# The fifth mixing product in one pass of fp32r over exact high and low parts, with the tanh values in the keys' buffer

## What is computed

```python
xx = x_prev - x
mix = jnp.tanh((x + xx * time_maa_x) @ maa_w1).reshape(b, t, 5, E_MIX)   # E_MIX = 32
mix = jnp.einsum('btfe,fec->fbtc', mix, maa_w2)
mw, mk, mv, mr, mg = mix
xw = x + xx * (time_maa_w + mw)      # likewise xk, xv, xr, xg
r = xr @ Wr.T;  k = xk @ Wk.T;  v = xv @ Wv.T
g = jax.nn.silu(xg @ Wg.T)
```

## Time and profile before

| what | us |
|---|---|
| median of 3 runs (lowest, highest) | 3530.97 (3509.68, 3533.42) |
| the profiled execution: time, span | 3509.35, 3507.2 |
| TensorE, VectorE, ScalarE, GpSimd busy | 3143.1, 2473.1, 1897.2, 784.9 |
| mean granted clock of TensorE | 0.983 |
| keys' buffer K1 in one tile: last read (state product, L542) starts | 1749.80 |
| tanh values are written to TMA (L782), TMB (L784) | 1764.16, 1766.00 |
| keys are written to K1 again (L653) | 1790.41 |
| setup: GpSimd's subtraction over two weight blocks (L847) takes | 2.40 |

### The profile page before, as it was taken

One profiled execution on the slowest core, in us unless ns is written; L12 is line 12 of the kernel. 1 busy time (PEld: TensorE's weight loads), 2 busy tenths in 40 slices (PEclk: granted clock), 3 DMA queues, 4 the chain that ended last, 5 costly groups with the idle time before them and its releaser, 6 DMA issues.

```text
span 3507.2 us, 98753 instructions
## 1 busy us (share of the span) xinstructions
PE 3143.1 (90%) x39261; PEld 2257.9 (64%) x39261; DVE 2473.1 (71%) x5108; ACT 1897.2 (54%) x3852; POOL 784.9 (22%) x725
## 2 busy tenths in 40 slices
PE   1899999999999999999999999999999999999997
PEld 0566666766666766666666666766666766666764
DVE  8466686776676676776766776676786776677776
ACT  0445556645566555566555566555566655556653
POOL 3122211122221122221222221222211122221121
PEclk9899999999999999999999999999999999999998
DMA  4000000000000000000000000000000000000000
GB/s 184 14 8 19 20 14 17 17 14 20 14 17 20 17 14 20 14 17 20 17 14 20 14 17 20 17 14 20 14 19 18 17 20 14 20 14 17 20 17 13
DMA packets 22598, 73.04 MB, mean 21 GB/s; under 512 B 3041, under 2 KB 3297, under 8 KB 20545
## 3 DMA queue, kind: packets, MB, share of 16 engines
q1 hardware_dynamic: 22208, 66.76, 5.4%
HBM read 49.97 MB, written 16.78 MB: 19 GB/s over the span
## 4 chain that ended last, share of the span: by engine, by line
PE 25%; DVE 22%; issue 21%; ACT 19%; POOL 10%; POOLq 1%; DMA 1%; ACTq 1%; DVEq 0%; SPq 0%
PE psP L393 7%; ACT ARENA L653 7%; PE psP L423 6%; ACT HHI L810 6%; POOL MT L856 5%; POOL ARENA L870 4%; PE psF L615 4%; ACT GG L801 3%; DVE ARENA L1125 3%; DVE ARENA L1087 3%; DVE ARENA L1077 2%; DVE HLO L1237 2%; DVE SUMS L1229 2%; DVE GR L1245 2%; PE psX L375 1%
## 5 line engine op out<-in xcount | busy, mean ns | idle before, releaser
L393 PE MATMUL psP<-ARENA,WALL 128*128 128x256 f32 x3072 | 692.0, 382 | 0.2 <-ACT ARENA L684 0.2
L653 ACT ACTIVATE ARENA<-ARENA 32x512 f32<-32x512 f32 (+1 forms) x992 | 578.8, 583 | 189.8 <-DVE ARENA L1077 137.7
L393 PEld LDWEIGHTS psP<-ARENA,WALL 128*128 128x128 f32 x3072 | 574.6, 190 | 84.5 <-issue 11.3
L1237 DVE SCALAR_TENSOR_TENSOR HLO<-GG,FWB,HHI 128x128 f16<-128x128 f32 x1024 | 292.3, 347 | 459.8 <-ACT HHI L810 455.7
L615 PE MATMUL psF<-XHI,WFC 128*128 128x128 f16 x4096 | 490.0, 220 | 46.5 <-DVE XLO L1216 34.0
L615 PE MATMUL psF<-XLO,WFC 128*128 128x128 f16 x4096 | 488.8, 220 | 0.0
L615 PEld LDWEIGHTS psF<-XHI,WFC 128*128 128x128 f16 x4096 | 401.7, 99 | 88.1 <-issue 86.0
L615 PEld LDWEIGHTS psF<-XLO,WFC 128*128 128x128 f16 x4096 | 402.9, 98 | 14.0 <-issue 10.3
L870 POOL TENSOR_TENSOR ARENA<-ARENA,XT 128x1024 f32<-128x1024 f32 x128 | 285.2, 2228 | 507.4 <-DVE ARENA L1029 507.4
L634 PE MATMUL psF<-WPJ,HHI 128*128 128x512 f16 x1024 | 389.8, 381 | 3.1 <-ACT GG L801 3.1
L634 PE MATMUL psF<-WPJ,HLO 128*128 128x512 f16 x1024 | 388.1, 379 | 0.0
(11 more groups left out here) (166 smaller groups left out, 5418.0 us busy)
## 6 DMA issues: line engine op xcount, KB each, us to landing
XT<-x_ch SPq DMA_DIRECT2D x33, 520.0 KB, 3.4
ARENA<-x_tok SPq DMA_DIRECT2D x32, 512.0 KB, 4.1
out<-OUT SPq DMA_DIRECT2D x64, 256.0 KB, 2.0
WALL<-w_all SPq DMA_DIRECT2D x5, 1024.0 KB, 16.6
ARENA<-wfc SPq DMA_DIRECT2D x4, 1024.0 KB, 7.9
ARENA<-wpj SPq DMA_DIRECT2D x3, 1024.0 KB, 14.6
GG<-wpj SPq DMA_DIRECT2D x1, 1024.0 KB, 18.6
OUT<-w2a SPq DMA_DIRECT2D x8, 64.0 KB, 14.9
```

The lines of the kernel that those rows point to most:

```text
L393: mm = pe.matmul(psP[:, P.bank(f"{name}{g}"), COLS * c:COLS * (c + 1)], WALL[:, w, k, 128 * (2 * g + c):128 * (2 * g + c + 1)], cc(XF[slot ...
L653: return act.activation(o, i, ACT.Copy)
L1237: e = dve.scalar_tensor_tensor(out=HLO[:, k, :], in0=GG[:, u % 2, 0, 128 * m:128 * (m + 1)], scalar=FWB[:, 0, k:k + 1], in1=HHI[:, k, :], ...
```

## The change

The fifth mixing is treated as the other four. W2S and MT get a fifth block, W2B and the f32 matmul go; `mix` has one form. ScalarE's `mix_high` now waits for both tanh values, rounds TMB too (into TMBH), and makes ten copies in place of eight; GpSimd's `mix_low` makes ten subtractions in place of eight and waits for both roundings. The counts of the semaphores follow. TMA, TMH, TMB and TMBH all lie in K1. In the setup, the fifth weight block is loaded four times (into V) where it was loaded once, and GpSimd makes one cast and one subtraction more, over one block.

```diff
--- before.py
+++ after.py
@@ -109,10 +109,9 @@
 
         WALL = sb("WALL", [128, 5, KC, C])
         W1 = sb("W1", [128, KC, 5 * MIXR])
-        W2S = sb("W2S", [128, 4, C], F32R)
+        W2S = sb("W2S", [128, 5, C], F32R)
         TD1 = sb("TD1", [128, KC, DECR])
-        TD2W2 = sb("TD2W2", [DECR + MIXR, C])
-        TD2, W2B = TD2W2[0:DECR, :], TD2W2[DECR:DECR + MIXR, :]
+        TD2 = sb("TD2", [DECR, C])[:, :]
         PAR = sb("PAR", [128, KC, NPAR])
         WFC = sb("WFC", [128, KC, HID], F16)
         WPJ = sb("WPJ", [128, MH, C], F16)
@@ -139,7 +138,8 @@
         A = ARENA1[:, 6144:7168]
         RSX = A.rearrange("p (q n) -> p q n", q=PAIRS)
         K1 = ARENA1[:, 7168:8192]
-        TMH = K1[:, 0:COLS]
+        TMA, TMH = K1[:, 0:COLS], K1[:, COLS:2 * COLS]
+        TMB, TMBH = K1[0:MIXR, 2 * COLS:3 * COLS], K1[0:MIXR, 3 * COLS:4 * COLS]
         KT = ARENA1[:, 7168:8192].rearrange("p (q n) -> p q n", q=PAIRS)
         S = ARENA2[:, 0:512].rearrange("p (c b n) -> p c b n", b=B, c=KC)
         XF = [ARENA2[:, 512 + 1024 * i:1536 + 1024 * i] for i in range(2)]
@@ -152,11 +152,9 @@
 
         XT = sb("XT", [128, KC * B, CH + 1])
         XX = sb("XX", [128, KC * B, CH])
-        TMA = sb("TMA", [128, COLS])
-        MTALL = sb("MT", [128, 4, COLS], F32R)
-        MT = [MTALL[:, f, :] for f in range(4)]
-        TZTM = sb("TZTM", [DECR + MIXR, COLS])
-        TZ, TMB = TZTM[0:DECR, :], TZTM[DECR:DECR + MIXR, :]
+        MTALL = sb("MT", [128, 5, COLS], F32R)
+        MT = [MTALL[:, f, :] for f in range(5)]
+        TZ = sb("TZ", [DECR, COLS])[:, :]
         TOT = {1: D}
         for n in (2, 4, 8, 16, 32, 64):
             TOT[n] = sb(f"TOT{n}", [128, KC * COLS // n])[:, :]
@@ -189,7 +187,7 @@
         RAW = ([ARENA1[:, 2048 * k:2048 * (k + 1)] for k in range(4)] + [ARENA2[:, 2048 * k:2048 * (k + 1)] for k in range(3)]
                + [GG[:, :, :, :].rearrange("p i s n -> p (i s n)")])
 
-        W2RAW = (OUT[:, 0:2, :], X1[:, 0:2, :])
+        W2RAW = (OUT[:, 0:2, :], X1[:, 0:2, :], V[:, 0:1, :])
         psP = ctx.enter_context(nc.psum_tensor("psP", [128, 2, 512], F32))
         psW = ctx.enter_context(nc.psum_tensor("psW", [128, 2, 512], F32))
         psX = ctx.enter_context(nc.psum_tensor("psX", [128, 512], F32))
@@ -257,7 +255,7 @@
                     halves(RM[rows(h), :], n)[1].rearrange("p (c q) n -> p c q n", c=KC))
 
         NPL = len(LEVELS) + 2
-        NWEIGHTS = 8 + 4 * 4
+        NWEIGHTS = 7 + 5 * 4
         POOL_PARTS = (2, 5, 7)
 
         def over_tiles(eng, attention, feed_forward):
@@ -282,12 +280,12 @@
                 sp.dma_start(RAW[4 + k], wpj[:, 2048 * k:2048 * (k + 1)]).then_inc(raw_in[4 + k], 16)
             sp.dma_start(XT[:, :, :], x_ch[0]).then_inc(xt_in, 16)
             sp.dma_start(WALL[:, W_V, :, :], w_all[:, W_V, :, :]).then_inc(values_in, 16)
-            for dst, src in ((W1[:, :, :], w1), (W2B[:, :], w2b), (TD1[:, :, :], td1),
+            for dst, src in ((W1[:, :, :], w1), (TD1[:, :, :], td1),
                              (TD2[:, :], td2), (WALL[:, W_K, :, :], w_all[:, W_K, :, :])):
                 sp.dma_start(dst, src).then_inc(weights_in, 16)
-            for f in range(4):
+            for f in range(5):
                 for copy in range(4):
-                    sp.dma_start(W2RAW[f // 2][rows(copy), f % 2, :], w2a[rows(f), :]).then_inc(weights_in, 16)
+                    sp.dma_start(W2RAW[f // 2][rows(copy), f % 2, :], w2a[rows(f), :] if f < 4 else w2b).then_inc(weights_in, 16)
             for w in (W_R, W_G, W_O):
                 sp.dma_start(WALL[:, w, :, :], w_all[:, w, :, :]).then_inc(weights_in, 16)
 
@@ -363,12 +361,9 @@
 
             def mix(t, f, name, wait_free):
 
-                if f < 4:
-                    pe.wait_ge(mt_high, 4 * (t + 1) + f + 1)
-                    pe.wait_ge(mt_low, 8 * (t + 1) + 2 * f + 2)
-                else:
-                    pe.wait_ge(tm_ready, M.read(t, "w1b"))
-                lhs, rhs = (W2S[:, f, :], MT[f]) if f < 4 else (W2B[:, :], TMB[:, :])
+                pe.wait_ge(mt_high, 5 * (t + 1) + f + 1)
+                pe.wait_ge(mt_low, 10 * (t + 1) + 2 * f + 2)
+                lhs, rhs = W2S[:, f, :], MT[f]
                 for g in range(2):
                     wait_free(f"{name}{g}")
                     for c in range(2):
@@ -376,7 +371,7 @@
                                        lhs[:, 128 * (2 * g + c):128 * (2 * g + c + 1)], rhs, start=True, stop=True)
                     mm.then_inc(m_full, 1)
 
-            pe.wait_ge(w2_split, 4)
+            pe.wait_ge(w2_split, 6)
             mix(-1, 0, "mw", lambda name: None)
 
             def tile(it, first, ffn):
@@ -654,11 +649,13 @@
 
             def mix_high(t):
 
-                act.wait_ge(tm_ready, M.read(t, "w1a"))
+                act.wait_ge(tm_ready, M.read(t, "w1b"))
                 copy(TMH.bitcast(F32R), TMA[:, :]).then_inc(tm_rounded, 1)
-                for f in range(4):
-                    copy(MT[f][rows(0), :], TMA[rows(f), :])
-                    copy(MT[f][rows(2), :], TMA[rows(f), :]).then_inc(mt_high, 1)
+                copy(TMBH.bitcast(F32R), TMB[:, :]).then_inc(tm_rounded, 1)
+                for f in range(5):
+                    src = TMA[rows(f), :] if f < 4 else TMB
+                    copy(MT[f][rows(0), :], src)
+                    copy(MT[f][rows(2), :], src).then_inc(mt_high, 1)
 
             act.wait_ge(su_dve, 6)
             act.wait_ge(su_pool, 2)
@@ -691,7 +688,7 @@
                 if not first:
                     act.wait_ge(x_full, X.full(it - 1, "kv1"))
                     act.wait_ge(p_dve, P.read(it - 1, "wo1"))
-                act.wait_ge(mt_low, 8 * (it + 1))
+                act.wait_ge(mt_low, 10 * (it + 1))
                 for g in range(2):
                     act.wait_ge(p_full, P.full(it, f"k{g}"))
                     src = psP[:, P.bank(f"k{g}"), :]
@@ -838,25 +835,26 @@
             pool.wait_ge(su_pool, 2)
 
             pool.wait_ge(weights_in, 16 * NWEIGHTS)
-            for i in range(2):
+            for i in range(3):
                 if i:
-                    pool.wait_ge(w2_split, 2)
-                w = W2S[:, 2 * i:2 * (i + 1), :]
+                    pool.wait_ge(w2_split, 2 * i)
+                w = W2S[:, 2 * i:min(2 * i + 2, 5), :]
                 pool.tensor_copy(w, W2RAW[i]).then_inc(w2_split, 1)
                 pool.wait_ge(w2_split, 2 * i + 1)
                 pool.tensor_tensor(w[64:128, :, :], W2RAW[i][64:128, :, :], w[64:128, :, :].bitcast(F32), ALU.subtract).then_inc(w2_split, 1)
 
             def mix_low(t):
 
-                pool.wait_ge(tm_rounded, t + 2)
-                for n in range(8):
+                pool.wait_ge(tm_rounded, 2 * t + 4)
+                for n in range(10):
                     if n:
-                        pool.wait_ge(mt_low, 8 * (t + 1) + n)
+                        pool.wait_ge(mt_low, 10 * (t + 1) + n)
                     f = n // 2
-                    pool.tensor_tensor(MT[f][rows(1 + 2 * (n % 2)), :], TMA[rows(f), :], TMH[rows(f), :], ALU.subtract).then_inc(mt_low, 1)
-                pool.wait_ge(mt_low, 8 * (t + 1) + 8)
-
-            pool.wait_ge(w2_split, 4)
+                    whole, high = (TMA[rows(f), :], TMH[rows(f), :]) if f < 4 else (TMB, TMBH)
+                    pool.tensor_tensor(MT[f][rows(1 + 2 * (n % 2)), :], whole, high, ALU.subtract).then_inc(mt_low, 1)
+                pool.wait_ge(mt_low, 10 * (t + 1) + 10)
+
+            pool.wait_ge(w2_split, 6)
             mix_low(-1)
 
             def inverse_root(v):
```

## The result

| | before | after |
|---|---|---|
| median of 4 runs, us | 3531.43 (3509.68 to 3533.42) | 3443.71 (3442.45 to 3448.73) |
| profiled execution, us | 3509.35 | 3442.92 |
| its span, us | 3507.2 | 3441.1 |

What follows compares the result with a forecast made beforehand. TensorE, busy 90% of the span, was taken to bound the kernel, with the chain running through mg. 3483.9 without clock falls, less 47.0 for mg, plus 8.5 for five falls, gave 3445.4 us; range 3433 to 3471.

Steps and rivals of the forecast that it cites:

- The base: Profiled time of the kernel before without its 15 low-clock stretches of 1.70 us at the output product: 3483.9 us.
- The saving at mg: Fifth mixing product on TensorE, as quick as mr: 2.07 to 0.60 us, saving 1.47 us in each of 32 tiles, 47.0 us.
- The low end of 1.35: mg's saving per tile counted from the first record of each product instead: 1.92 - 0.57 us, 43.2 us over 32 tiles.
- All of it on the path: Receptance behind mg finds its input and bank ready, with some 1 us to spare, so the whole saving counts.
- ScalarE and GpSimd at no cost: Added 1.3 us on ScalarE and 1.58 on GpSimd per tile fit idle time; GpSimd's root keeps 3.9 us to spare.
- VectorE beside GpSimd: VectorE is not held beside the added subtractions: cost 0; if L1193 were held, 0.83 us a tile, 26.6 us.
- Setup at no cost, 3 us to either side: Extra weight loads, cast and subtraction in setup fit idle time: cost 0, give or take 3 us for first-tile low clock.
- Five falls: Output product behind TensorE's 1.88 us wait: clock drops to 1.2 GHz, 1.70 us each, in about 5 tiles, 8.5 us.
- the first (a fall in every tile): Low clock at the output product in nearly all tiles, since the wait is untouched: 3487.9 us; chance 0.10.
- The second (half the gain caught at receptance): Values' bank or VectorE's work late ahead of receptance or the scaled queries, losing 23.5 us: 3469 us; chance 0.08.
- the third (the product isn't what mr is): New mg costs as much as before, nothing gained: about 3531 us; chance 0.02.
- The fourth, a second fall behind a wait: Lighter TensorE work around mg lets the clock drop there too, two drops a tile: 3545.7 us, slower; chance 0.02.

Runs made afterwards that it cites:

- experiment 1: Kernel before, with seven needless f16 matmuls per tile ahead of TensorE's wait for the gated output: 3484.25 us, ratio 0.986.
- experiment 10: Changed kernel with seven needless matmuls in the wait, mg one pass over 32 rows of rounded values and weights, remainders left out: 3443.52 us, ratio 0.9774 to before.
- experiment 2: Changed kernel with seven needless f16 matmuls per tile ahead of TensorE's wait for the gated output: 3433.91 us, ratio 0.9712 to the kernel before.
- experiment 4: Changed kernel with all its added roundings, copies and subtractions, but mg kept full f32 over 32 rows: 3530.67 us, ratio 0.9983 to the kernel before.
- experiment 5: Changed kernel with seven needless matmuls in the wait, MT's fifth block written only in setup, so tiles keep eight copies and subtractions: 3434.68 us, ratio 0.9755 to before.
- experiment 6: Changed kernel with seven needless matmuls in the wait and four more GpSimd subtractions per tile: 3439.56 us, ratio 0.9765 to the kernel before.
- experiment 7: Changed kernel with seven needless matmuls in the wait and eight more GpSimd subtractions per tile: 3531.93 us, ratio 1.002 to the kernel before.
- experiment 9: Kernel before, with four of the last down-projection's eight matmuls moved ahead of the wait for the gated output: median 3482.26 us, 3480.49 without one outlier, ratio 0.9888.
- experiment 8: Changed kernel with four of the last down-projection's eight matmuls moved ahead of the wait for the gated output: 3434.74 us, ratio 0.9755 to the kernel before.
- experiment 3: Changed kernel with eight needless matmuls (1.62 us) right behind mg, restoring the old tile length: 3524.56 us, ratio 0.9995 to the kernel before.
- experiment 11: Changed kernel with half the last down-projection moved into the gated-output wait, plus four needless one-column matmuls there: 3430.51 us, ratio 0.9743 to the kernel before.

## Why the prediction was right

Its sum gave 3445.4 with a range of 3433 to 3471, and 3443.71 was measured. By its own steps:

- **The base.** Right: 3483.9 against 3484.25 in experiment 1.
- **The saving at mg.** The mechanism was right, the size a little low: 1.47 us a tile were counted, and undisturbed tiles are 104.12 - 102.52 = 1.60 us closer. Of the 0.13 us that were missed, 0.10 is receptance, which takes 2695.07 - 2688.16 = 6.91 us up to the next product's start instead of 7.01. The forecast took the time between two neighbours but stopped at the second one's start, though the neighbour itself is longer behind a product over 32 rows (7.17 in the earlier trace rows and in experiment 10, 7.07 in experiment 2). The low end of 1.35 was off in the wrong direction.
- **All of it on the path.** Right: 0.2 us of waiting ahead of L388 in the whole run.
- **ScalarE and GpSimd at no cost.** Right, by experiments 4 and 5. The slack of 3.83 us was forecast as 3.9, and experiments 6 and 7 put its end between four and eight more subtractions. VectorE beside GpSimd was also forecast as free; experiment 6 shows that it can be slowed there, by 0.08 us at L1040 and 0.24 at L1202. In the kernel after, neither is met by the subtractions: L1191 takes 0.69 us beside the added pair, as L1193 did in the earlier trace rows.
- **Setup at no cost, 3 us to either side.** The cost is right, the 3 us to either side were too few. The distance from the first output product to the second went from 288.34 - 180.60 = 107.74 us to 101.61, which is 4.5 more than one mg accounts for. The granted clock in it was 0.94 before and is 0.98 now. So the first tile has less of the low clock, and that lies outside of the 3 us. It isn't the change that brings it: experiment 9 has it with the instructions of the kernel before (103.43 us), and experiment 2, with the whole change and the matmuls in the wait, lacks it (286.68 - 180.66 = 106.02). The moments at which the low stretches come differ from execution to execution; what sets them is open.
- **Five falls.** Right to the count in the profiled execution, which is luck; the reason given has support. That the wait makes them is shown by experiments 1, 2, 8 and 9, in which it is shortened and they are gone from the output product. That the spacing has a part in how many there are is shown by experiment 3, where the old spacing brings 26 back. It can't be the spacing alone, since tiles 104.12 us apart without a fall stand beside tiles 105.82 apart with one in the same execution. Why a fall wants the moment that it wants was not tried. The 28 falls that the forecast gave to the median before were worked out with a first tile of 107.74 us; with the short one of experiment 9 it would be 3531.43 - 3479.6 = 51.8 us, or 30 to 31 falls, as the 31 of experiment 4 at 3532.01. No trace shows the median execution.

The sum, made anew for the profiled execution, with 31 mg, since the first stands ahead of the first output product, which starts at 180.68 as it did at 180.60: 3509.35 - 15 x 1.70 (falls before) - 31 x 1.60 (mg) - 4.5 (first tile) = 3429.8; + 5 x 1.70 (falls left) = 3438.3; measured 3442.92. The remaining 4.6 us are the step that the prediction did not have, the gaps in the bursts. The 30 distances from the second tile on give about the same: 3087.25 - 4 x 1.70 = 3080.45 us against 3075.09 in experiment 2, so 5.4. The three tiles that fall behind in L509 have 0.82 + 0.37 + 0.66 = 1.85 us of that over 102.52, so about 3.5 are left for the state product. So the forecast's three errors nearly cancel, which is luck too: mg gives 49.6 us instead of 47.0, the first tile gives 4.5 instead of 0, the gaps take 4.6 to 5.4 instead of 0.

The gain of 87.7 us between the medians can be made up in two ways. With the long first tile in the median before it is 23 x 1.70 = 39.1 (28 falls, 5 now) + 49.6 (mg) + 4.5 (first tile) - 5.4 (gaps) = 87.8. With the short one it is 26 x 1.70 = 44.2 (31 falls, 5 now) + 49.6 - 5.4 = 88.4. Both fit, and the change's own work is the 49.6 in both; the rest is to be had without the change, by experiments 1 and 9.

Of the rivals, the first (a fall in every tile) did not come, yet experiment 3 is almost that rival, at the old spacing. The second (half the gain caught at receptance) and the third (the product isn't what mr is) are refuted by the rows of L370 and L388. The fourth, a second fall behind a wait, did not come from the change, but experiment 7 shows the clock fall once a new wait stands ahead of a long product.

What stays open: what makes TensorE stand still in the two bursts. The table of experiment 11 shows that a gap keeps its place in the code, and that more matmuls ahead of it put it into another part of the work; experiment 8 (a regrouping) leaves it where it was. That TensorE lacks instructions there is the reading of "issue" and was only argued; no run looked at the fetching of the code, nor at why a gap is 0.35 us in one tile and 0.91 in another. For experiment 10, that a change of the row count between neighbours costs about 0.1 us ahead of mg and as much in the product behind it is what the rows show, and why it does is open.

## What to carry to other kernels

Before a small gain is credited to an edit, count what comes and goes by itself: here 1.70 us of low clock behind a wait, in 5 tiles or in some 30, decide over 39 to 44 us, and a few matmuls that had to be done anyway, moved into that wait, removed them from the long product at both spacings. When an f32 product over few rows is replaced by one over stacked parts, price it from its neighbours' starts, the one behind included, and take the work that prepares it from idle time whose end is known: 3.83 us of cover took 3.2 us of additions almost freely (2.9 us in all), and 6.3 us cost 98.

## What the hardware showed unexpectedly

- Idle time inside a burst of short matmuls that no engine ends: the longest distance of two starts in the state product is 0.35 to 0.47 us in most tiles after and 0.6 to 0.9 in eight, but 0.08 in most tiles before and in experiment 2. Gaps of 0.36 us leave the tile's length as it is, those of 0.42 to 0.47 add 0 to 0.2 us to it, and longer ones up to half a microsecond. A gap has a fixed place in the code: 14, 8 or 24 records put in ahead of the burst let it come 14, 8 or 24 records earlier.
- One pass over 32 rows between neighbours over 128 is 0.35 us a tile slower than over 128 rows, although it multiplies a quarter.
- A fall costs according to where it lies: 1.70 us in a long f32 product, nothing that could be read at the short products behind mw in experiments 8 and 9.
- The first tile took 107.74 us in one execution and 103.43 in another, by a longer stretch of the low clock over the same instructions.
